# First pass of a graph network layer on one core: the edge product as two full-height matmuls of 512 columns in place of four half-height ones of 256

## What is computed

```python
h = relu(layernorm(x))
e = concatenate([h[src], batch[src], edge_attr], axis=1)     # 128 + 1 + 64 features
m = relu(batchnorm(e @ W1 + b1))                             # 256 features an edge
agg = segment_mean(m, dst)                                   # a row for each node
h2 = relu(batchnorm(concatenate([h, batch, agg], axis=1) @ W2 + b2))
out = x + relu(h2 @ W3 + b3)
```

## Time and profile before

| | before |
|---|---|
| median of three runs | 3292.05 us (3285.0 to 3298.05) |
| the profiled execution | 3268.36 us |
| its span, first to last instruction | 3266.6 us |
| mean granted TensorE clock | 0.824 |
| busy: PE, DVE, POOL, ACT | 2494.8, 1807.0, 1755.0, 973.6 us |
| POOL's gathers of table rows | 1581 |
| moved by DMA | 741.36 MB, mean 227 GB/s |
| table stage, first pass, second pass and end | to 190, 190 to 2520, 2520 to 3267 us |

### The profile page before, as it was taken

One profiled execution on the slowest core, in us unless ns is written; L12 is line 12 of the kernel. 1 busy time (PEld: TensorE's weight loads), 2 busy tenths in 40 slices (PEclk: granted clock), 3 DMA queues, 4 the chain that ended last, 5 costly groups with the idle time before them and its releaser, 6 DMA issues.

```text
span 3266.6 us, 42293 instructions
## 1 busy us (share of the span) xinstructions
PE 2494.8 (76%) x14769; PEld 1082.0 (33%) x14769; DVE 1807.0 (55%) x5121; ACT 973.6 (30%) x1601; POOL 1755.0 (54%) x1847
## 2 busy tenths in 40 slices
PE   1467777774777777777777777777777899999998
PEld 1332332222323323323322232223232444444448
DVE  2444444455545444444444454444444899889878
ACT  1321221121222212221222121222212555565546
POOL 7246666666666666666666666666665222222220
PEclk7778877887777777777787788777787999999999
DMA  6356666665666666666666666566565999999965
GB/s 180 126 181 202 217 201 205 219 214 170 219 214 218 205 200 210 208 200 212 206 207 214 198 219 206 192 209 213 194 217 196 344 342 342 343 345 342 343 246 158
DMA packets 270664, 741.36 MB, mean 227 GB/s; under 512 B 46391, under 2 KB 98661, under 8 KB 270448
## 3 DMA queue, kind: packets, MB, share of 16 engines
q1 hardware_dynamic: 189152, 525.28, 44.9%
q0 software_dynamic: 78432, 212.46, 22.1%
q10 hardware_dynamic: 2864, 0.86, 0.1%
HBM read 501.63 MB, written 236.81 MB: 226 GB/s over the span
## 4 chain that ended last, share of the span: by engine, by line
PE 58%; issue 17%; another core or an unknown queue 7%; POOL 6%; DVE 5%; DMA 4%; ACT 1%; SPq 0%; DVEq 0%; POOLq 0%; ACTq 0%
PE psum L1224 16%; PE psum L1177 11%; PE psum L1318 6%; POOL sums L562 6%; PE psum L1337 6%; PE psum L1190 4%; DMA late<-m_d 3%; PE psum L1180 2%; PE psum L1179 2%; PE psum L1178 2%; PE psum L1348 2%; PE psum L1403 2%; DVE sums L966 1%; PE psum L1279 1%
## 5 line engine op out<-in xcount | busy, mean ns | idle before, releaser
L562 POOL DMA_INDIRECT sums<-P_d,late x1581 | 1504.0, 951 | 900.2 <-issue 452.5
L966 DVE TENSOR_TENSOR sums<-psum,sums 128x1024 f32<-128x1024 f32 x396 | 482.9, 1219 | 974.2 <-remote 826.6
L650 ACT ACTIVATE sums<-sums 128x1024 f32<-128x1024 f32 x416 | 438.6, 1055 | 1733.6 <-remote 1172.1
L1224 PE MATMUL psum<-late,sums 64*128 64x256 f32 x3320 | 707.9, 469 | 294.4 <-issue 241.1
L1224 PEld LDWEIGHTS psum<-late,sums 64*128 64x128 f32 x3320 | 384.2, 218 | 827.5 <-issue 705.8
L1177 PE MATMUL psum<-sums,ones 128*32 128x512 f32 x830 | 539.8, 730 | 70.6 <-issue 64.8
L1180 PE MATMUL psum<-sums,ones 128*32 128x512 f32 x830 | 537.8, 725 | 44.8 <-issue 42.5
L1178 PE MATMUL psum<-sums,ones 128*32 128x512 f32 x830 | 546.3, 738 | 29.8 <-issue 28.0
L1179 PE MATMUL psum<-sums,ones 128*32 128x512 f32 x830 | 541.3, 731 | 35.3 <-issue 33.7
L929 DVE TENSOR_SCALAR late<-late 128x98 bf16<-128x98 bf16 x1661 | 441.7, 278 | 178.3 <-remote 142.1
L1007 DVE TENSOR_TENSOR late<-late,psum 128x1024 f32<-128x1024 f32 x416 | 492.9, 1213 | 36.6 <-DMA late<-m_d 32.6
(11 more groups left out here) (187 smaller groups left out, 1985.1 us busy)
## 6 DMA issues: line engine op xcount, KB each, us to landing
m_d<-sums SPq DMA_DIRECT2D x415, 512.0 KB
late<-m_d SPq DMA_DIRECT2D x415, 512.0 KB, 5.4
sums<-in_ea_main SPq DMA_DIRECT2D x103, 512.0 KB
sums<-P_d,late POOLq DMA_INDIRECT x1581
P_d<-sums SPq DMA_DIRECT2D x24, 512.0 KB, 2.9
nodes<-in_x SPq DMA_DIRECT2D x24, 256.0 KB
late<-in_x SPq DMA_DIRECT2D x24, 256.0 KB, 3.3
out<-late SPq DMA_DIRECT2D x24, 256.0 KB, 2.5
```

The lines of the kernel that those rows point to most:

```text
L562: pool.indirect_dma_start(out=m_s[s][0:r, k * L:(k + 1) * L], out_offset=None, in_=P1_d, in_offset=bass.IndirectOffsetOnAxis(ap=idx[0:r, G ...
L966: dve.tensor_tensor(m_s[s][0:r, 0:w], ps_m[place_m[g]][0:r, 0:w], m_s[s][0:r, 0:w], ALU.add).then_inc(s_m, 1)
L1224: ins = pe.matmul(ps_m[place_m[g]][:, k * L:(k + 1) * L], ea[lo:lo + EF, a:a + P], W1c[lo:lo + EF, :], start=True, stop=g not in xg_no, sk ...
```

## The change

Host: the 64 attributes of tiles 0 and 2 of a group lie on the lower 64 partitions and those of tiles 1 and 3 on the upper ones, so that 128 neighbouring columns of ea_main hold a pair of tiles. SBUF: W1c becomes 128 x 512, with W1c in its upper left and lower right quarter and zeros in the others. One matmul of 128 rows and 512 columns then gives two tiles at once, a bank of PSUM wide; there are two a group. In groups without gather the products with W1a follow behind each of the two. POOL clears the two quarters ahead of its other constants (new semaphore s_zero), and DVE's sign product covers 512 columns and waits for it.

```diff
-        W1c = late[:, at:at + L]
-        at += L
+        W1c = late[:, at:at + 2 * L]
+        at += 2 * L
...
-        assert at <= 1024 * M2_SLOTS + 6 * L and 3 * EW <= 1024 * M2_SLOTS
+        assert at <= late.shape[1] and 3 * EW <= 1024 * M2_SLOTS
...
+        s_zero = sem("s_zero")
...
-                                 (W1c[0:EF, :], W1[NF + 1:, :]), (W1c[EF:, :], W1[NF + 1:, :])]:
+                                 (W1c[0:EF, 0:L], W1[NF + 1:, :]), (W1c[EF:, L:], W1[NF + 1:, :])]:
...
+            pool.memset(W1c[0:EF, L:], 0.0).then_inc(s_zero, 1)
+            pool.wait_ge(s_zero, 1)
+            pool.memset(W1c[EF:, 0:L], 0.0).then_inc(s_zero, 1)
+            pool.wait_ge(s_zero, 2)
...
-            dve.tensor_tensor(W1c[:, :], W1c[:, :], sgn[:, :], ALU.mult).then_inc(s_sgn, 1)
+            dve.wait_ge(s_zero, 2)
+            half_W1c = W1c.rearrange("p (r f) -> p r f", r=2)
+            dve.tensor_tensor(half_W1c, half_W1c, sgn.unsqueeze(1).to_broadcast([P, 2, L]), ALU.mult).then_inc(s_sgn, 1)
...
-                    for k in (0, 2, 1, 3):
-                        lo, a = EF * (k // 2), (k % 2) * P
-                        ins = pe.matmul(ps_m[place_m[g]][:, k * L:(k + 1) * L], ea[lo:lo + EF, a:a + P], W1c[lo:lo + EF, :],
+                    for i in range(2):
+                        ins = pe.matmul(ps_m[place_m[g]][:, 2 * i * L:2 * (i + 1) * L], ea[:, i * P:(i + 1) * P], W1c[:, :],
                                         start=True, stop=g not in xg_no, skip_group_check=True)
-                        if g in xg_no and k >= 2:
-                            for i in (k - 2, k):
-                                ins = pe.matmul(ps_m[place_m[g]][:, i * L:(i + 1) * L], xg[xg_no[g]][:, i, :], W1a[:, :],
+                        if g in xg_no:
+                            for k in (2 * i, 2 * i + 1):
+                                ins = pe.matmul(ps_m[place_m[g]][:, k * L:(k + 1) * L], xg[xg_no[g]][:, k, :], W1a[:, :],
                                                 start=False, stop=True, skip_group_check=True)
...
-                    ins = pe.matmul(ps_m[place_m[g]][0:r, 0:L], ea_t[:, :], W1c[0:EF, :], start=True, stop=True)
+                    ins = pe.matmul(ps_m[place_m[g]][0:r, 0:L], ea_t[:, :], W1c[0:EF, 0:L], start=True, stop=True)
...
-    ea_main = spread(ea).reshape(full // GE, 2, HALF, f).transpose(1, 3, 0, 2).reshape(2 * f, full // 2)
+    ea_main = spread(ea).reshape(full // GE, 2, 2, P, f).transpose(2, 4, 0, 1, 3).reshape(2 * f, full // 2)
```

## The result

| | before | after |
|---|---|---|
| median of five runs | 3292.05 us (3285.0 to 3298.05) | 3263.85 us (3259.62 to 3271.92) |
| ratio, 95% interval | | 0.9919 (0.9901 to 0.9936) |
| the profiled execution | 3268.36 us | 3263.35 us |
| mean granted TensorE clock | 0.824 | 0.863 |

The change made the kernel faster by 0.8%, 28 us; 3388 us, 3% slower, was forecast. The profiled execution of before lies 17 us under the lowest of its timed runs, so the two traces are only 5 us apart. They show how the time is made up, but not where all 28 us went.

The account below looks back on a forecast made before the run. PE was taken as scarce in free stretches, its progress setting POOL's stops. 25.0 more stops of 3.8 us gave +95 us, with setup +96: 3268.4 to 3364 us, 3388 on the runs' scale; range 3230 to 3460.

Parts of the forecast that it names:

- What the change costs the array: PE's edge product in the first pass: 1.07 to 1.82 us, +0.72 us a group at full clock.
- What lies in the rest: Gathers still cost 1.24 us with issue, other stages stay as they were, setup adds 0 to 1.5 us, taken as 1.
- Groups per cycle: Free plus paced stretch in the first pass: 4.31 groups fall to 3.42, 25.0 more POOL stops, +95 us.
- the length of the free stretch: First-pass time in which PE issues without the 0.70 us step; held fixed at 11.46 us.
- the prediction's own equation: First pass: groups a cycle n = 2.86 + (4.72n + 3.8 - 11.46)/15.0, giving 3.42.
- The row that I used for the length: DVE's prologue operations start 0.71 us apart beside POOL's gathers; read as a series of gathers bringing paced issue on.
- the sign of hidden time: In the first pass, POOL's waits staying at 371 us would show PE's time hidden; about 466 was forecast.
- the sign of instructions: In the first pass, free stretches lengthening past 15 us would show that PE's instruction count ends them.
- fewer instructions delay the paced stretch: First pass: a free stretch ends after 73 PE records, so 17.0 stops fewer, -64 us, 3229 us; chance 0.16.
- My objection to the rival: In the prologue DVE shows the same issue step when PE has little to do, against a count of PE instructions.
- the clock pays it back: Denser PE work holds 2.4 GHz through first-pass free stretches: 3.37 us a group, 3301 us, no change; chance 0.08.
- PE's time is hidden: First pass: POOL's stops follow from the gather queue alone, PE catches up, nothing moves, 3292 us; chance 0.13.

Follow-up runs that it names:

- e5: The changed kernel with only the first of a group's four tiles gathered, on chip 5: 2290.53 us, a single run.
- e1: The changed kernel with its edge product cut into four full-height products of 256 columns, on chip 5: 3296.32 us, 1.0031 of the kernel before.
- e6: The changed kernel plus four one-column bf16 products a group on PE, on chip 5: 3292.71 us, 1.0022 of the kernel before.
- e3: The changed kernel plus eight one-column copies a group on ACT, on chip 5: 3286.38 us, 0.9998 of the kernel before.
- f4: The kernel before with the counts of only one of four tiles, on chip 12: 2845.24 us, 0.9996 of the kernel before.
- f1: The change as it is against the kernel before, on chip 12: 2847.02 us, 1.0005.

## Where the prediction held and where it failed

**What the change costs the array: right.** Forecast 3.13 us a free group at full clock, measured 3.14 in after and in e5; 0.72 us more than 2.42, as in the sum. Within it the edge product takes 1.92 us in the chain, not 1.82, and the counts 0.23, where the earlier trace rows had 0.36: the chain draws the border between them elsewhere, and their sum went from 1.43 to 2.15 us, by 0.72. The overhead of every matmul that the Trainium skill gives (TensorEngine Tiling (Array Packing), section Instruction Overhead) doesn't show on these wide products: four records fewer would have taken 0.1 us off that (an estimate from the page), and e1 with four more takes 0.02 us more. On products of one column it does: e6's four cost 0.12/4 = 0.03 us each.

**What lies in the rest: right.** The gather costs 951 ns in both traces, the second pass stayed at 747 us, and setup is too small to show.

**Groups per cycle: the step that failed.** "I hold the length of the free stretch fixed, since it begins with POOL's restart and the paced issue came with gathers." Measured, it went from 11.26 to 14.46 us, 28% longer, and from 8.6 to 11.1 gathers. With the length fixed a more costly group means fewer groups a cycle, 2.86 in a free stretch, hence 121 stops. With a fixed number of recorded instructions instead, a group that has 8 of them fewer means more groups and more gathers a cycle. There were 91 paced stretches, and 97 before. Put the measured length and clock into the prediction's own equation: a free group takes 3.14/0.90 = 3.49 us, 14.46/3.49 = 4.14 groups, n = 4.14 + (4.72n + 3.8 - 14.46)/15.0 = 5.0, 83 cycles, 13 fewer, -50 us. Measured were -28, so the equation still takes too much, but it has the sign. The length is the larger part of the error, but not all of it: with the measured length and the forecast's 4.01 us a group the equation gives 98 cycles and +8 us, with the forecast's length and 3.49 us a group 103 cycles and +24 us. So the clock of the free stretches, taken as 0.84 and measured as 0.90, was the second term that was off. The row that I used for the length, says that gathers must be there for pacing; e5 bears that out. It says nothing of what counts towards it, and I read it as if it did.

**The prediction's own signs.** POOL's waits stayed near 371 us (381 as the profile divides them, 369 as gaps of over 1 us), which was the sign of hidden time, and the free stretches came to 14.46 us, just short of the 15 that were the sign of instructions. The two traces alone don't decide between these; e1, e3 and e6 do as far as it is shown: with the array time of the change and the instructions put back, chip 5 shows 0 to 12 us of loss, and the change stands 0.8 to 1.1% below them.

**The rival "fewer instructions delay the paced stretch": right in sign, wrong in what is counted.** It got 0.16 and -64 us. I counted PE's records alone, 73 a stretch. e3 shows that ACT's copies cost too (0.8%, where PE's instructions cost 1.0 and 1.1%), and PE's share of a free stretch goes from 140 to 112 while the count of all engines stays at 190 to 201 in five kernels. My objection to the rival, that DVE was paced when PE had little to do, tells only against a count of PE's instructions, not against one over all engines.

**The rival "the clock pays it back": the clock rose, and its own worth is not shown.** The clock in free stretches rose from 0.82 to 0.90, in the stage from 0.78 to 0.83. The Trainium skill's rule (TensorE: Matmul & The Clock Gate, section Why this matters for your kernels) that sustained activity brings the full clock agrees with that. But f4 and f1 take the same time at 0.77 and 0.89 where POOL never stops, and on chip 5 e1, at a mean clock of 0.871, takes 12 us longer than the kernel before. Every run on chip 5 has both the longer group and the higher clock, so none tells what the rise gives back.

**The rival "PE's time is hidden": right on the other chips.** There the first pass is 1581 gathers of 0.95 us with gaps of 0.3 us, and PE's 3.14 us lie under the 5.0 us of a group. I gave it 0.13, since I took the paced stretches for a property of the kernel. The runs show them as a property of kernel and chip together.

**Where the time of a paced chip goes, as far as shown.** From before to e1, which has before's instructions and the change's array time, +0.3% or 12 us on chip 5. From e1 to the change, 8 instructions fewer a group, 1.1% or 36 us by the two ratios, the second of which is from another measurement. Six stops fewer of 3.8 us are 23 us by the counts of the traces, of the same size. As the profile divides POOL's idle time, after has 10 us more of stops than before; by the gaps of over 1 us it has 8 us less, against 5 us between the two executions. Where the rest of the 28 us lies, the two traces can't show.

**Open.** Whether it is the number of recorded instructions that ends a free stretch, or something that goes with it: five kernels of two measurements are all there is, and the runs meant to take instructions away or to double the dose fell on chips without pacing. How much of the loss of e1 and e6 comes from the groups in paced stretches. What the change gives on chip 5. Why chip 5 is paced and 9, 12 and 1 are not. Whether the pacing is there at all when no profile is taken: every timed execution has records of its engines, so no run here tells.

## What to carry to other kernels

When a stretch of a trace repeats, ask separately what must be present for it to end and what is counted until it ends; a length that is held fixed because its cause is known is an assumption with its own rival. Where an engine's instruction starts are evenly spaced, put a few instructions without effect on an idle engine: that tells a count from a cost. And when a small gain rests on such stretches, time it on more than one chip: this one was 0.8% in the result's measurement and nothing on chip 12, whose traces have next to none.

## What the runs showed of the hardware

- The same kernel takes 3284.5 us on chip 5 and 2846 to 2847 us on chips 9, 12 and 1. Between the traces of before and of f1 some 77 us of that lie in the table stage (the first gather of table rows starts at 187 and at 110 us) and some 347 us in the first pass (2327 and 1981 us from its first gather to its last). Paced stretches, in which PE's instructions start about 0.70 us apart, fill 1051 us of before's first pass and next to nothing of f1's. DVE's show that step in the table stage; POOL's gathers keep their 1.25 us in it.
- With paced stretches, a free one holds 190 to 201 recorded instructions of all engines in the mean of five kernels, whatever its length (11.3 to 14.5 us), its gathers (8.6 to 11.1) and PE's share (112 to 140). Without three quarters of the first pass's gathers there is no paced stretch in it (e5).
- DVE operations of 685 and 559 ns on bf16 with broadcast operands, in place of eight of 0.28 us, lengthen an indirect gather on POOL from 948 to 998 and 1002 ns.
- A first pass with POOL at its bound takes the same time at a granted clock of 0.77 and 0.89.
